# A two-model graph network on one core: row sums moved to ScalarE, Wd2's halves made in the last layer, decoder transposes one tile later

## The reference

```python
def L0(x):
    h = layernorm(x, ln_in_g, ln_in_b)
    h = relu(h @ W1 + b1) @ W2 + b2                       # 1024 -> 512 -> 256
    for i in range(3):
        z = h + segment_sum(h[src], dst)
        z = relu(z @ Wa[i] + ba[i]) @ Wb[i] + bb[i]
        h = h + relu(layernorm(z, ng[i], nb[i]))
    delta = relu(h @ Wd1 + bd1) @ Wd2 + bd2               # 256 -> 512 -> 1024
    return layernorm(x + delta, out_g, out_b)
def L1(x):                                                # twice, relu between
    mean = segment_sum(h[src], dst) / max(deg, 1)
    h = h @ W_self + mean @ W_neigh + b
x = norm(x + L0(x)); x = norm(x + L1(x))
```

## Time and profile before

| | us |
|---|---|
| median of three runs | 1065.68 |
| the profiled execution | 1068.29 |
| its span | 1066.5 |
| TensorE busy | 999.7 (94%) |
| VectorE busy | 532.8 (50%) |
| ScalarE busy | 351.3 (33%) |
| GpSimd busy | 260.7 (24%) |
| mean granted clock of TensorE | 0.982 |

### The profile page before, as it was taken

The page is one execution under the profiler, slowest core; times in us unless marked ns, Lnnn a source line. Parts: engine busy times, 40 slices in busy tenths (PEclk is TensorE's granted clock), DMA queues, the critical chain, the costliest instruction groups (busy, mean ns, idle before and its releaser), DMA issues.

```text
span 1066.5 us, 14810 instructions
## 1 busy us (share of the span) xinstructions
PE 999.7 (94%) x4862; PEld 809.2 (76%) x4862; DVE 532.8 (50%) x1314; ACT 351.3 (33%) x632; POOL 260.7 (24%) x320
## 2 busy tenths in 40 slices
PE   4788999989897998999999999999999999999996
PEld 2366778879786787887777887778887777887774
DVE  7998965364568986332222332212234233335545
ACT  4555643152435576321112221113431011222221
POOL 3000003751325431724005234005216003300000
PEclk9699999999999999999999999999999999999999
DMA  6167682993003584315123104234325335103444
GB/s 203 58 105 209 172 193 68 208 206 72 20 1 139 183 291 140 128 38 161 68 102 111 37 25 156 74 135 128 108 88 167 121 102 165 41 1 127 150 134 133
DMA packets 48263, 127.13 MB, mean 119 GB/s; under 512 B 17775, under 2 KB 18784, under 8 KB 48016
## 3 DMA queue, kind: packets, MB, share of 16 engines
q1 hardware_dynamic: 33622, 74.91, 23.6%
q0 software_dynamic: 8288, 37.29, 12.9%
q10 hardware_dynamic: 6298, 14.21, 3.9%
HBM read 101.76 MB, written 45.13 MB: 138 GB/s over the span
## 4 chain that ended last, share of the span: by engine, by line
PE 81%; DVE 8%; ACT 4%; issue 3%; DMA 1%; POOL 1%; SPq 0%; ACTq 0%; DVEq 0%; POOLq 0%
PE bank L1734 41%; PE bank L1755 17%; PE bank L623 5%; PE bank L1075 5%; PE bank L1107 4%; PE bank L587 3%; PE bank L1434 3%; DVE wide L961 1%; DVE wide L963 1%; PE bank L1448 1%; ACT xt_f L257 1%; DMA w_f<-W_pairs 1%; PE bank L1415 1%; DMA x_rows<-x 1%; POOL h_f L809 1%
## 5 line engine op out<-in xcount | busy, mean ns | idle before, releaser
L1674 DVE TENSOR_TENSOR h_stage<-h_turned,h_stage 128x1000 fp32r<-128x1000 f32 x80 | 103.9, 1299 | 371.7 <-ACT h_stage L1600 371.7
L1734 PE MATMUL bank<-w_self,h_stage 128*125 128x512 f32 x960 | 229.5, 394 | 0.0
L1734 PE MATMUL bank<-w_neigh,h_stage 128*125 128x512 f32 x960 | 227.2, 397 | 0.1
L1734 PEld LDWEIGHTS bank<-w_self,h_stage 128*125 128x125 f32 x960 | 177.9, 185 | 44.9
L1734 PEld LDWEIGHTS bank<-w_neigh,h_stage 128*125 128x125 f32 x960 | 178.1, 187 | 44.1 <-issue 0.3
L1755 PE MATMUL bank<-g_rows,a_stage 125*125 125x512 f32 x800 | 192.7, 395 | 0.0
L1600 ACT ACTIVATE h_stage<-h_turned 128x1000 fp32r (+1 forms) x80 | 83.9, 1048 | 306.6 <-PE bank L1734 294.2
L1755 PEld LDWEIGHTS bank<-g_rows,a_stage 125*125 125x125 f32 x800 | 148.5, 186 | 37.7
L1565 POOL CAST w_self<-w_stage 128x512 fp32r<-128x512 f32 x32 | 22.8, 712 | 230.0 <-PE bank L1734 221.7
L1107 PE MATMUL bank<-a_turned,gn 125*128 125x418 f32 x360 | 70.5, 354 | 3.0 <-DVE gn L967 3.0
L1107 PEld LDWEIGHTS bank<-a_turned,gn 125*128 125x128 f32 x360 | 67.0, 188 | 4.5 <-DVE gn L967 3.6
(11 more groups left out here) (210 smaller groups left out, 1118.7 us busy)
## 6 DMA issues: line engine op xcount, KB each, us to landing
a_stage<-at_dram SPq DMA_DIRECT2D x40, 625.0 KB, 4.0
w_stage<-w_self POOLq DMA_DIRECT2D x32, 256.0 KB, 3.1
at_dram<-a_turned SPq DMA_DIRECT2D x10, 625.0 KB, 9.5
w_stage<-w_neigh POOLq DMA_DIRECT2D x24, 256.0 KB, 2.9
dec_y<-x_bd SPq DMA_DIRECT2D x10, 512.0 KB, 4.1
dec_x<-x_ob SPq DMA_DIRECT2D x10, 512.0 KB, 5.0
x_dram<-h_rows SPq DMA_DIRECT2D x10, 512.0 KB, 3.6
h_dram<-o ACTq DMA_DIRECT2D x20, 256.0 KB
```

The source lines that it names most:

```text
L1674: dve.tensor_tensor(st[u][:, 1, :, :], ht[:, :, bass.ds(t * NT, NT)], raw(st[u][:, 0, :, :]), ALU.subtract).then_inc(st_ready, 1)
L1734: mm = pe.matmul(out, st[u][:, a, k, :], w[:, b, k * 512:(k + 1) * 512], start=(k == 0 and p == 0), stop=(k == KD - 1 and p == 2))
```

## The change

It has four parts.

1. For pairs 1 to 4 the rows' sums are made on ScalarE (`row_moments`): a copy with a running sum for each of the pair's two tiles, then, once VectorE has scaled the sums (`means`), a square of the deviations with a running sum; VectorE makes the variance from it (`variances`) and, after the fifth group of masks, the normalizer. Pair 0 keeps its statistics on VectorE. In ScalarE's queue `affine(p, 0)` now stands ahead of the root, and the sums between them.
2. The picks, which say which chunk of edges a window's mask is made from, are made in two products, the first pair's first, and the table step behind them is cut in the same way (`first_chunks`).
3. Wd2's halves are made in the last layer: `wd2_high(j)` ahead of the relu of chunk j on ScalarE, the four subtractions at the front of GpSimd's part of that layer. They lie in a place of their own (`wd2`), and the wide product's rows in another (`z1`). SyncE's loads for the decoder now wait for the last layer's second product.
4. The decoder's transposes and their evacuation come three tiles behind the product instead of two.

```diff
+        def row_moments(p):
+            act.wait_ge(xhat_read, 2 * p - 1)
+            for u in range(2):
+                act.wait_ge(x_in[u], 16 * (p + 1))
+                ...
+                act.activation(xhat[0][0:NT, :], x_rows[u][0:NT, :], ACT.Copy, accum_out=row_sum[0:NT, u:u + 1])\
+                   .then_inc(sums_ready, 1)
+            act.wait_ge(mean_ready, p)
+            for u in range(2):
+                ...
+                act.activation(xhat[0][0:NT, :], x_rows[u][0:NT, :], ACT.Square, bias=minus_mean[0:NT, u:u + 1],
+                               accum_out=row_squares[0:NT, u:u + 1]).then_inc(squares_ready, 1)
...
         for p in range(1, PAIRS):
             read_counts(p - 1)
+            affine(p, 0)
             if p + 1 < PAIRS:
+                row_moments(p + 1)
                 take_root(p + 1)
-            affine(p, 0)
             relu(p - 1, 0)
...
+        def means(p):
+            dve.wait_ge(sums_ready, 2 * p)
+            dve.wait_ge(norm_ready, p)
+            dve.tensor_scalar(minus_mean[0:NT, :], row_sum[0:NT, :], -1.0 / D, None, ALU.mult).then_inc(mean_ready, 1)
+
+        def variances(p):
+            dve.wait_ge(squares_ready, 2 * p)
+            dve.wait_ge(norm_ready, p)
+            dve.tensor_scalar(var_eps[0:NT, :], row_squares[0:NT, :], 1.0 / D, EPS, ALU.mult, ALU.add).then_inc(var_ready, 1)
...
                 if p == 0:
+                    if j == 0:
+                        first_chunks(slice(GROUP, WINDOWS), ps_z1[0], 2)
                     if j == 1:
                         w1_low(1)
                         norm_low(0, 0)
                     if j == 2:
-                        statistics(1)
                         w1_low(2)
                         w1_low(3)
+                        means(1)
                     if j == 3:
                         norm_low(0, 1)
-                        normalizer(1)
+                        variances(1)
                 else:
-                    if j == 0 and p + 1 < PAIRS:
-                        normalizer(p + 1)
                     if j == 2:
                         norm_low(p, 0)
+                        if p + 1 < PAIRS:
+                            means(p + 1)
+                    if j == 3 and p + 1 < PAIRS:
+                        variances(p + 1)
+                if j == 4 and p + 1 < PAIRS:
+                    normalizer(p + 1)
...
             if p > 0:
                 norm_low(p, 1)
-            if p + 2 < PAIRS:
-                statistics(p + 2)
...
-        choose(ps_counts[3], VW, lambda j: pick[0:EP, j, :]).then_inc(picks, 1)
+        choose(ps_counts[3], GROUP * VISITS, lambda j: pick[0:EP, j, 0:GROUP * VISITS]).then_inc(picks, 1)
+        choose(ps_z1[0], VW - GROUP * VISITS, lambda j: pick[0:EP, j, GROUP * VISITS:VW]).then_inc(picks, 1)
...
         sp.wait_ge(x_summed, 16 * 2 * T)
+        sp.wait_ge(b_mm, T * LAYERS)
...
+            if last:
+                for k in range(KH):
+                    hi, lo = [s.wd2[:, h, k * D:(k + 1) * D] for h in range(2)]
+                    pool.wait_ge(wd_hi, k + 1)
+                    pool.tensor_tensor(lo, wd_f32[k % 3][:, :], raw(hi), ALU.subtract).then_inc(wd_ready, 1)
...
-            chunks(0, 4)
+            for j in range(4):
+                if last:
+                    wd2_high(j)
+                chunks(j, j + 1)
...
         for j in range(KH, KH * NCH):
-            if j % 2 == 0:
-                wd2_high((j - KH) // 2)
             z1_relu(j)
...
         for t in range(T - 2):
-            if t >= 2:
-                fill(act, t - 2)
+            if t >= 3:
+                fill(act, t - 3)
...
         for t in range(T):
             product(t)
-            if t >= 2:
-                turn(pe, t - 2)
+            if t >= 3:
+                turn(pe, t - 3)
+        turn(pe, T - 3)
```

More of the change, by code:

```diff
@@ L160, in graph_block @@
     iota = at("iota", [128, KEYS], F16)
+    row_sum, row_squares, minus_mean = [at(n, [128, 2], F32) for n in ("row_sum", "row_squares", "minus_mean")]
     assert at.at <= nc.sbuf_usable_end, at.at - nc.sbuf_usable_end
@@ L402, in normalizer @@
             newton_rstd(dve, norm_step, 5 * p, rstd[0:NT, :], var_eps[0:NT, :], root[0:NT, :], scratch[0:NT, :])
-            dve.scalar_tensor_tensor(out=shift[0:NT, :], in0=mean_var[0:NT, :, 0], scalar=-1.0, in1=rstd[0:NT, :],
-                                     op0=ALU.mult, op1=ALU.mult).then_inc(norm_ready, 1)
+            if p == 0:
+                dve.wait_ge(stat_step, 7)
+            else:
+                dve.wait_ge(mean_ready, p)
+            dve.tensor_tensor(shift[0:NT, :], minus_mean[0:NT, :], rstd[0:NT, :], ALU.mult).then_inc(norm_ready, 1)
         def visit(n, g, v):
@@ L456, in w1_low, with first_chunks @@
             dve.tensor_tensor(lo, w_f32[n][:, :], raw(hi), ALU.subtract).then_inc(w_ready, 1)
+        def first_chunks(own, found, part):
+            dve.wait_ge(picks, part)
+            width = own.stop - own.start
+            dve.tensor_tensor(tab[0:EC, :, own, :], found[0:EC, 0:2 * width * VISITS].rearrange("p (q g v) -> p q g v", q=2,
+                              g=width), offsets[0:EC, :, own, :], ALU.subtract).then_inc(tab_ready, 1)
+            dve.wait_ge(tab_ready, part)
         dve.memset(ones[:, :], 1.0).then_inc(ones_set, 1)
@@ L517, in _ @@
         dve.tensor_copy(chunk_ids[0:EP, :], table[0:EP, 0:2]).then_inc(row_step, 1)
-        statistics(0)
+        statistics()
         w1_low(0)
         normalizer(0)
-        dve.wait_ge(picks, 1)
-        dve.tensor_tensor(tab[0:EC, :, :, :].rearrange("p q g v -> p (q g v)"), ps_counts[3][0:EC, 0:2 * VW],
-                          offsets[0:EC, :, :, :].rearrange("p q g v -> p (q g v)"), ALU.subtract).then_inc(tab_ready, 1)
-        dve.wait_ge(tab_ready, 1)
+        first_chunks(slice(0, GROUP), ps_counts[3], 1)
         dve.wait_ge(row_step, 5)
@@ L842, in _ @@
         over_layers(pool, layer)
-        pool.wait_ge(h_ready, T * LAYERS)
-        for k in range(KH):
-            hi, lo = [s.w_self[:, h, k * D:(k + 1) * D] for h in range(2)]
-            pool.wait_ge(wd_hi, k + 1)
-            pool.tensor_tensor(lo, wd_f32[k % 3][:, :], raw(hi), ALU.subtract).then_inc(wd_ready, 1)
     @block.scalar
@@ L1041, in split_wide @@
             k, c = j % KH, j // KH
-            hi, lo = [s.wide[:, hl, k, c * CH:(c + 1) * CH] for hl in range(2)]
+            hi, lo = [s.z1[:, hl, k, c * CH:(c + 1) * CH] for hl in range(2)]
             split(ZD + j, hi, lo, z1_out[j % 4][:, :])
@@ L1433, in product @@
                     for p, (a, b) in enumerate(HALVES):
-                        mm = pe.matmul(y_banks[t % 2][c][0:NT, :], s.wide[:, a, k, t * NT:(t + 1) * NT],
-                                       s.w_self[:, b, k * D + 512 * c:k * D + 512 * c + 512],
+                        mm = pe.matmul(y_banks[t % 2][c][0:NT, :], s.z1[:, a, k, t * NT:(t + 1) * NT],
+                                       s.wd2[:, b, k * D + 512 * c:k * D + 512 * c + 512],
                                        start=(k == 0 and p == 0), stop=(k == KH - 1 and p == 2))
@@ L1656, in _ @@
         s.normalize(act, T - 1)
+        s.fill(act, T - 2)
         stage(0, 1, 1)
+        tile(0, 0, 1)
         s.fill(act, T - 1)
-        tile(0, 0, 1)
         act.wait_ge(s.ht_filled, 2 * T)
```

31 lines of the change are left out of this document (20 added, 11 removed).

## The result

| | before | after |
|---|---|---|
| median, us | 1066.92 (1064.64 to 1068.92, 6 runs) | 1060.77 (1057.29 to 1061.89, 6 runs) |
| ratio | | 0.9939, 95% interval 0.9919 to 0.9959 |
| span of the profiled execution | 1066.5 | 1059.1 |
| mean granted clock | 0.982 | 0.983 |

A forecast was written before the change was run, and what follows sets the result against it. TensorE was taken as the bound (81% of the chain), so only its waits and low clock pay. Gains 2.5 + 0 + 8.4 + 0.6 = 11.5 us took the median from 1065.68 to 1054.2; range 1048.5 to 1060.5.

The forecast's parts named there:

- the seam: Between encoder and decoder: without GpSimd's Wd2 subtractions there, first decoder tile read at 343.9 instead of 352.37, 8.4 us gained.
- the clears: At the seam: GpSimd's clears (1.84 and two of 0.1 us) delay VectorE's twelve splits from 342.0 to 343.9.
- the cycles of the second and third pair: Graph stage: 23.5 us undisturbed plus new TensorE stalls of 0.9 and 1.7 make 26.1 instead of 27.9.
- I take 2.5: Gain forecast for the graph stage from part 1, row sums on ScalarE; bounds 9.7 us gained to 2.0 lost.
- if they pass 28: Sign that the prediction is wrong: the graph stage's loop cycles take more than 28 us.
- Rival B: Graph stage: new stalls let TensorE's clock fall in all three cycles, 2.0 us lost instead of 2.5 gained, 1058.7; 16%.
- Rival D: Slower: graph-stage clock stays low through the rest of each cycle; at 5 us lost per cycle 1069; 3%.
- I take 0: Last layer: making Wd2's halves there (part 3) was forecast to cost nothing.
- the bad end: Last layer: one lockout of VectorE by GpSimd on the path of the second product's third tile, 2.4 us lost.
- The last layer has grown: Sign that the prediction is wrong: the last encoder layer takes longer than before.
- Rival C: Seam stays late, or GpSimd's work lands on the last layer's path: part 3 gives 1 to 5, 1059 to 1062; 6%.
- Rival A: Graph stage: ScalarE's queue hides the sums after all, 9.7 us gained instead of 2.5, 1047.0; 8%.

The follow-up runs named there:

- experiment 5: Kernel of experiment 4, with each of GpSimd's four Wd2 subtractions also waiting for VectorE's split of the same number: 1061.46 us, ratio 0.9930 to before.
- experiment 11: Kernel of experiment 4 plus experiment 9's wait, first encoder weights loaded early, Wd2 subtractions 0 to 2 behind splits 0 to 2, fourth behind split 2: 1056.39 us, ratio 0.9889.
- experiment 2: Kernel before with parts 3 and 4 of the change alone, graph stage as before: 1060.24 us, ratio 0.9921 to before.
- experiment 1: Kernel before with parts 1 and 2 of the change alone, all else as before: 1068.82 us, ratio 1.0008 to before.
- experiment 4: Changed kernel with ScalarE's first two relus ahead of the squares and the next pair's normalize behind later relus and z1's copy: 1052.98 us, ratio 0.9858 to before.
- experiment 9: Kernel of experiment 4, with GpSimd's first two copies of x waiting until the last pair's rows have landed: 1058.04 us, ratio 0.9911 to before.
- experiment 3: The changed kernel run again with nothing altered: 1060.09 us, ratio 0.9923 to before.

## Why the prediction was right, and where it was not

**Right: the seam.** 9.04 gained, 8.4 forecast. The mechanism is the one named: with GpSimd's subtractions elsewhere the casts are 0.37. The size is off by the clears, put at 1.9 and measured at 0.6. VectorE's splits therefore end 11.7 after their start instead of 13.0, and what sets the seam is the bound that was put below them: TensorE's first product, forecast to start 6.7 behind the first split and to end at 12.4, started 6.6 behind it and its tile was read at 12.45.

**Wrong: the cycles of the graph stage.** This step failed: "the cycles of the second and third pair are 23.5 + 0.9 + 1.7 = 26.1 instead of 27.9", "I take 2.5". Measured are 25.3, 26.5 and 28.2 (again: 25.4, 28.2, 26.6), and parts 1 and 2 alone gain nothing. The stalls are where they were forecast, for the reason that was given. Two sizes were off. The stall before the transposes is 1.85 to 2.0, not 1.5 to 1.7, and with small delays a cycle is 0.3 to 0.4 longer. And the clock: "the new stalls are shorter than the old one with the low clock" was taken as ground to leave its cost out. In each of three traces of this graph stage it fell once in three cycles, for 1.6 to 1.7. The four cycles took 2.5 us more than forecast (103.4 against 100.9): 0.3 + 0.4 + 0.4 for the stalls, 1.7 for the clock, less 0.3 in the last. The prediction's own sign, "if they pass 28", came with it: one cycle is 28.2 in each of these traces. Rival B had this mechanism, with all three cycles; it held for one. Rival D had the clock low through the rest of each cycle; no trace of the change shows that.

**Wrong: the last layer.** "I take 0" came out as 1.2. The lockout that was the bad end, 2.4 us, did happen, at the first split instead of the third tile, and TensorE's slack hid half of it. The step that failed is "VectorE has 2.79 us of idle time before a split there, so a lockout of 2.4 fits": that time lies ahead of the data. GpSimd's subtractions start when ScalarE's `hi` halves are ready, at 290.52 and 293.11, and so ran across the cast at 292.12. Experiments 5 and 11 show it from both sides: with the subtractions moved onto another instruction the layer is 48.9, with none in the way 45.4. "The last layer has grown" was among the signs named of a wrong prediction, and Rival C held a part of it ("its work lands on the last layer's path"), with the seam late as well, which it wasn't. (Its price is off too: part 3 at 1 to 5 instead of 8.4 gives 1057.6 to 1061.6, not 1059 to 1062.) The Trainium skill, "SBUF — State Buffer", section "SBUF: two separate sides", gives the rule: VectorE and GpSimd share a port pair; VectorE's instructions in a two-port mode need it, and those with two SBUF inputs do against a GpSimd instruction that reads SBUF; the one that starts first has it to its end, and the other fully blocks. The traces agree, down to an instruction on three columns that took 2.30 instead of 0.17, and a subtraction beside the clears, which read nothing, kept its 0.60. Which mode an instruction ran in no row shows.

**Too small: part 4.** 1.36 instead of 0.6. "One tile" is spared the evacuation by VectorE's first tiles, worth 0.9; besides, the three tiles after the fourth come every 6.3 on average instead of 6.43, and VectorE no longer waits 0.3 to 0.5 for TensorE's product ahead of each. The last ones come every 6.4 as before.

**Not in the sum: the layers ahead of the last.** They took 122.3 before, 124.2 and 122.2 after. No step of the change acts there; experiment 2 gives 122.5. In the first trace of the change the clock falls twice there, in the other three once (in experiment 1, with 124.8, three times).

Part 2 was put at nothing. It had no experiment of its own, and the first dense product starts anywhere from 47.3 to 49.6 in these traces whichever graph stage they have, so a few tenths could not be seen. That stays open.

As the range goes, luck had a part. The two terms that were too small (the seam by 0.6, part 4 by 0.8) made up for more than the last layer's 1.2, and the time stands at the edge of the range, on the side of B and C.

**Rival A** was given 8%: the sums hidden, 9.7 gained in the graph stage. It did not happen in this change, but experiment 4 is it: 9.7 less than the change in that stage, at the same work. The argument against it (mean behind eighteen masks, third relu behind the normalizer) was an argument about the order of two queues, not about ScalarE's time. The Trainium skill, "Perfetto Trace Analysis", section "Optimizing Scalar/DVE Operations", says that moving work to ScalarE may make sense when VectorE is saturated. By the order of the change the trace disagrees, by that of experiment 4 it agrees.

## What to carry to other kernels

When work moves onto an engine with an in-order queue, look for its waits on the round trip to the other engine and put everything that is already runnable ahead of each of them: the same instructions gave nothing or 9.7 us. When an operation is moved because it locks out another engine, follow it to its new place and look up what that engine does there, small instructions too. After a stage has been made faster, expect the next limits to be transfers: here the edits of experiments 4, 9 and 11 were each right in their own stretch and left TensorE waits of 2.90, 8.19 and 5.87 us in the next one.

## What the runs showed of the hardware

- GpSimd's subtraction holds up small instructions of VectorE as well as large ones: a cast (0.38) took 1.04, a subtraction (0.59) 2.75, a TENSOR_SCALAR on three columns 2.30. Additions that read a bank (0.41) and BATCH_NORM_STATS2 (0.43) beside the fourth subtraction (301.94, 2.39 us) kept their time.
- Beside two clears on GpSimd (2.08 us together) two casts took 0.77 and 0.58, and the subtraction between them kept its 0.60.
- On ScalarE a copy of 1024 columns with a running sum took 1.04 and its read-out 0.19, together as long as the activation with scale and bias without a sum (1.23); a square took 1.15 and 0.19.
- The clock fell behind some stalls of 1.9 to 2.0 us and not behind others of the same length in the same kernel (behind 1.97 but not behind 2.10 in experiment 3), and the change's two traces differ in the places.
- A load of 512 KB landed in 3.5 to 3.7 us where the copies of x waited for it (experiment 9) and in up to 14.4 (experiment 5) beside two copies of 1.7 MB from memory to memory and the stored counts.
